# Feed-forward second products one by one in the bank of the sums, and a reordered beginning

## What is computed

```python
h = layernorm(x) * (1 + ca) + sa            # sa, ca, ga, sb, cb, gb: 6 vectors per batch, from silu(c) @ wmod
# attention: causal; each row's scores are first softmaxed within windows of 128 keys,
# and the probabilities so made go through a second softmax over all 1024 keys
x = x + ga * (softmax(window_softmax(q @ k.T / 4)) @ v @ Wo.T + bo)
h = layernorm(x) * (1 + cb) + sb
y = square(relu(h @ Wfc.T)) @ Wproj.T       # 256 -> 1024 -> 256
# five steps: mem = 0.9 * mem + y - (mem > 1);  out = number of steps with mem > 1
x = x + gb * count / 5
```

## Time and profile before

| | |
|---|---|
| median of 3 executions | 2550.83 us (2547.81 to 2559.81) |
| the profiled execution, its own time | 2552.97 us |
| its span from first to last instruction | 2551.1 us |
| mean granted TensorE clock | 0.981 |
| busy: PE, PEld | 2268.9 us (89%), 1266.0 us (50%) |
| busy: DVE, ACT, POOL | 1778.0 us (70%), 1566.2 us (61%), 876.6 us (34%) |
| chain that ended last | PE 70%, DVE 15%, ACT 10%, issue 3%, DMA 1% |

### The profile page before, as it was taken

One profiled execution on the slowest core, in us unless ns is written; L12 is line 12 of the kernel. 1 busy time (PEld: TensorE's weight loads), 2 busy tenths in 40 slices (PEclk: granted clock), 3 DMA queues, 4 the chain that ended last, 5 costly groups with the idle time before them and its releaser, 6 DMA issues.

```text
span 2551.1 us, 46605 instructions
## 1 busy us (share of the span) xinstructions
PE 2268.9 (89%) x19196; PEld 1266.0 (50%) x19196; DVE 1778.0 (70%) x2173; ACT 1566.2 (61%) x2450; POOL 876.6 (34%) x868
## 2 busy tenths in 40 slices
PE   4788889999899998999999998999989998889878
PEld 2434344555455554455544654455545555446537
DVE  4677886777866677876767777667777667777442
ACT  1377676665766567665666657666576656665632
POOL 1243134332533335322443225423253232232324
PEclk8999999999999999999999999999999999999979
DMA  6223122110321114011131013211032111110000
GB/s 187 77 65 106 28 65 85 53 49 12 101 76 28 49 36 127 28 43 36 49 110 53 24 30 93 65 53 49 12 114 63 28 36 32 53 28 7 6 28 17
DMA packets 112241, 140.21 MB, mean 55 GB/s; under 512 B 7912, under 2 KB 83848, under 8 KB 112032
## 3 DMA queue, kind: packets, MB, share of 16 engines
q1 hardware_dynamic: 112032, 137.22, 18.7%
HBM read 74.26 MB, written 58.74 MB: 52 GB/s over the span
## 4 chain that ended last, share of the span: by engine, by line
PE 70%; DVE 15%; ACT 10%; issue 3%; DMA 1%; POOL 0%; SPq 0%; ACTq 0%; POOLq 0%; DVEq 0%
PE sums L610 10%; PE score L555 9%; PE score L562 9%; PE pv L620 8%; PE score L597 8%; DVE negmax L909 7%; PE ring L575 6%; ACT e L805 5%; PE score L508 4%; PE score L525 4%; DVE e L926 4%; PE ring L651 3%; PE score L600 2%; DVE acc L971 1%; ACT qk_f L766 1%
## 5 line engine op out<-in xcount | busy, mean ns | idle before, releaser
L805 ACT ACTIVATE e<-score 128x512 f32<-128x512 f32 x1152 | 673.9, 596 | 343.9 <-PE score L600 206.2
L926 DVE TENSOR_TENSOR e<-ring,e 128x1024 f32<-128x1024 f32 x576 | 680.2, 1222 | 233.5 <-PE ring L651 233.2
L909 DVE TENSOR_REDUCE negmax<-ring 128x8 f32<-128x1024 f32 x512 | 607.3, 1219 | 194.4 <-PE ring L578 193.9
L810 ACT ACTIVATE e<-e 128x1024 f32<-128x1024 f32 x576 | 585.2, 1049 | 6.5 <-DVE e L926 6.1
L597 PE MATMUL score<-q_st,k_st 112*128 112x512 bf16 (+3 forms) x1536 | 462.4, 331 | 107.9 <-ACT qk_p L767 29.1
L575 PE MATMUL ring<-k_st,q_st 96*128 96x512 bf16 (+3 forms) x1536 | 374.7, 329 | 68.0 <-DVE negmax L909 24.0
L1155 POOL TENSOR_SCALAR r_h<-r_b,ab 128x256 bf16<-128x256 f32 x96 | 90.8, 946 | 892.0 <-DVE r_b L932 892.0
L610 PE MATMUL sums<-e,d_ones 128*32 128x256 f32 x4608 | 312.2, 389 | 23.5 <-ACT e L805 17.9
L620 PE MATMUL pv<-e,v 128*17 128x512 f32 (+3 forms) x3072 | 311.4, 494 | 2.9 <-ACT e L810 2.8
L597 PEld LDWEIGHTS score<-q_st,k_st 112*128 112x128 bf16 x1536 | 147.9, 97 | 321.5 <-issue 132.5
L555 PE MATMUL score<-hT,w_fc 128*128 128x256 f32 x1024 | 248.4, 387 | 4.6 <-ACT e L805 3.2
(11 more groups left out here) (123 smaller groups left out, 2521.8 us busy)
## 6 DMA issues: line engine op xcount, KB each, us to landing
q_st<-q_parts SPq DMA_DIRECT2D x32, 768.0 KB, 5.9
k_st<-k_parts SPq DMA_DIRECT2D x32, 768.0 KB, 8.6
q_parts<-qk_p SPq DMA_DIRECT2D x32, 384.0 KB, 2.6
k_parts<-qk_p SPq DMA_DIRECT2D x30, 384.0 KB, 2.6
x_in<-in_x SPq DMA_DIRECT2D x8, 1024.0 KB, 5.5
q_parts<-qk_p SPq DMA_DIRECT2D x32, 256.0 KB, 2.9
x_res<-in_x SPq DMA_DIRECT2D x8, 1024.0 KB, 6.1
out<-acc SPq DMA_DIRECT2D x32, 256.0 KB, 2.2
```

Source lines behind the costliest of these rows:

```text
L805: act.activation(e[:, n % ES, hh, :], score[SCORE_SLOT["st", n, hh][0]][:, :], ACT.Exp, scale=DK ** -0.5).then_inc(e1_done, 1)
L810: act.activation(v, v, ACT.Exp).then_inc(e2_done, 1)
L909: dve.tensor_reduce(negmax[:, hh, 8 * t:8 * t + 8], slot[:, :].rearrange("p (a n) -> p a n", n=P), AX_X, ALU.max, negate=True).then_inc(ri ...
L926: dve.tensor_tensor(v, ring[no % 2][:, :].rearrange("p (i n) -> p i n", i=2), v, ALU.mult).then_inc(ring_free, 1)
```

## The change

1. **F2 is gone as a piece.** Its 8 times 8 products a batch are single products (`quantum`), put by a table (`QUANTA`) at four places of 21 steps between step 22 and step 45 of the batch's back work, 1 to 3 at a place, 46 groups a batch. They accumulate in the right half of the `sums` bank. ACT copies each finished sum out (`take_sum`, 8 a batch); the next sum's first product waits for that copy, and so does the next `sum_unit`.
2. The table of pieces is split into `FRONT` and `BACK`, with other places. Back work now runs over up to 54 steps, so that its end lies in the next period: of a batch, 25 of the 64 products and 4 of the 16 F1 pieces lie beyond step 35.
3. **Spikes are counted on POOL** for all batches but the last, 9 instructions a chunk where DVE had 5. The last batch stays on DVE.
4. The second exponential is one instruction of 128x2048 where it was two. `products` now stand ahead of `sum_unit` in PE's step. POOL's inverse split writes its parts in place. One mask serves for both uses.
5. `x_res` is loaded in four parts, each as soon as the batch before has used its part; the gates are loaded in two; `load_x` comes two steps later.
6. **The beginning:** PE makes only the columns of the first norm ahead of T1; then all 8 QK and 4 V pieces; then the gates and the other columns; then the maxima. DVE splits the first four pieces before it makes the gates. SP stores these parts, loads the stacks of group 0 in two pairs of heads, and only then brings x of batch 1, the other parts and the feed-forward weights. POOL's first copies wait for the norm on DVE.

```diff
@@ tables
+QUANTA = {22: (3, 1, 0, 0), 23: (0, 0, 1, 1), 25: (1, 0, 2, 0), 26: (0, 2, 3, 0), 28: (0, 1, 0, 1), 29: (1, 1, 1, 2), 31: (2, 1, 1, 2), 32: (1, 0, 1, 0), 34: (1, 1, 1, 0), 35: (0, 1, 1, 2), 37: (1, 1, 0, 1), 38: (2, 0, 3, 0), 41: (1, 2, 0, 2), 43: (2, 2, 0, 0), 44: (1, 0, 1, 1), 36: (0, 0, 0, 1), 42: (0, 0, 2, 0), 30: (0, 0, 1, 0), 24: (0, 0, 1, 1), 45: (0, 0, 0, 1), 40: (1, 0, 0, 0)}
...
+def quanta(n):
+
+    out = [[], [], [], []]
+    for r, q in backs(n):
+        at = sum(sum(QUANTA[k]) for k in QUANTA if k < q)
+        for place, count in enumerate(QUANTA.get(q, ())):
+            for no in range(at, at + count):
+                out[place].append((r, no // (2 * NF), no // NF % 2, no % NF))
+            at += count
+    return out
+
+
+def sums_ended(n, place):
+
+    return [(r, c, i) for r, c, i, k in quanta(n)[place] if k == NF - 1]
...
+CHUNK_END = [max(q for q in QUANTA if sum(sum(QUANTA[k]) for k in QUANTA if k < q) < 2 * NF * (c + 1)) for c in range(4)]
+LN2_AT = {13: (0, 1), 14: (2, 3, 4, 5), 15: (6, 7)}
...
+PROLOGUE = [("T1", 0, n) for n in range(4)] + [("QK", 0, n) for n in range(8)] + [("V", 0, n) for n in range(4)]
@@ sync
+            for n in range(4):
+                store_parts(0, n)
+            for par in range(2):
+                sp.wait_ge(stored[par], 96)
+            for pair in range(2):
+                for stacked, dram in ((q_st, part_dram[0]), (k_st, part_dram[1])):
+                    sp.dma_start(stacked[0:KROWS, 0, 2 * pair:2 * pair + 2, :],
...
+            piece_full(sp, "T1", 0, 3)
+            load_x(1)
+            for n in range(4, 8):
+                store_parts(0, n)
...
                     for c in range(4):
+                        if q == max(4, CHUNK_END[c] + 4 - PERIOD):
+                            if r:
+                                sp.wait_ge(fin, 8 * (r - 1) + 2 * c + 2)
+                            sp.dma_start(x_res[:, 2 * c:2 * c + 2, :], x_rows[:, r, 2 * c:2 * c + 2, :]).then_inc(res_in[c], 16)
@@ tensor
-                elif kind == "F2":
-                    c, i = divmod(n, 2)
-                    for f in range(NF):
-                        if i == 0 and f % 2 == 0:
-                            pe.wait_ge(squared, 16 * r + 4 * c + f // 2 + 1)
-                        mm = pe.matmul(ps[:, 0:D], gT[:, f, P * i:P * i + P], w_proj[:, f, :], start=(f == 0), stop=(f == NF - 1))
                 mm.then_inc(piece_ready, 1)
+
+            def quantum(n, r, c, i, f):
+
+                if n % TRI == 0 or n > NUNIT:
+                    pe.wait_ge(r_newton, 2 * (min(n, NUNIT) // TRI - 1) + 1)
+                if f == 0 and (r or c or i):
+                    pe.wait_ge(back_evac, 8 * r + 2 * c + i)
+                if i == 0 and f % 2 == 0:
+                    pe.wait_ge(squared, 16 * r + 4 * c + f // 2 + 1)
+                mm = pe.matmul(sums[:, HALF:HALF + D], gT[:, f, P * i:P * i + P], w_proj[:, f, :],
+                               start=(n > NUNIT and f == 0), stop=(f == NF - 1), skip_group_check=True)
+                if f == NF - 1:
+                    mm.then_inc(back_sum, 1)
...
+                if BACK_ENDED[m + 1]:
+                    pe.wait_ge(back_evac, BACK_ENDED[m + 1])
...
+            for m in range(2):
+                col = 3 * D * m + 2 * D
+                for k in range(NT):
...
+            mm.then_inc(mod_product, 1)
+            columns_of(1)
             for k in range(len(TILES)):
+                if k == 1:
+                    pe.wait_ge(cols_ready, 2)
...
+                if 0 <= n - LAG_P < NUNIT:
+                    products(n - LAG_P)
                 if 0 <= n - 1 < NUNIT:
                     sum_unit(n - 1)
-                if 0 <= n - LAG_P < NUNIT:
-                    products(n - LAG_P)
...
+                for item in single[0]:
+                    quantum(n, *item)
...
+                for item in single[1]:
+                    quantum(n, *item)
@@ scalar
-                elif kind == "F2":
-                    c, i = divmod(n, 2)
-                    if r or c:
-                        act.wait_ge(lif, STEPS * (4 * r + c))
-                    act.activation(n1[:, D * i:D * i + D], ps[:, 0:D], ACT.Copy, scale=-1.0).then_inc(piece_evac, 1)
+
+            def take_sum(r, c, i):
+
+                act.wait_ge(back_sum, 8 * r + 2 * c + i + 1)
+                if i == 0 and (r or c):
+                    act.wait_ge(lif, counted(r, c))
+                act.activation(n1[:, D * i:D * i + D], sums[:, HALF:HALF + D], ACT.Copy, scale=-1.0).then_inc(back_evac, 1)
...
-            def second_exp(m, pair):
-                act.wait_ge(ring_free, RING_NO["r", m, pair] + 1)
-                v = e[:, m % ES, 2 * pair:2 * pair + 2, :]
+            def second_exp(m):
+                act.wait_ge(ring_free, RING_NO["r", m, 1] + 1)
+                v = e[:, m % ES, :, :]
                 act.activation(v, v, ACT.Exp).then_inc(e2_done, 1)
@@ vector
                 if k == 0:
-                    piece_done(dve, "F2", r, 2 * c + 1)
-                    if c == 0 and r + 2 < B:
-                        piece_full(dve, "BT", r + 2, 0)
-                    if r or c:
-                        dve.wait_ge(out_stored, 16 * (4 * r + c))
+                    dve.wait_ge(back_evac, 8 * r + 2 * c + 2)
+                    dve.wait_ge(out_stored, 16 * (4 * r + c))
@@ gpsimd
+            def count_spikes(r, c, k):
+
+                if k == 0:
+                    pool.wait_ge(back_evac, 8 * r + 2 * c + 2)
+                    if r or c:
+                        pool.wait_ge(out_stored, 16 * (4 * r + c))
+                    pool.tensor_scalar(acc[:, :], n1[:, :], -levels[k], None, ALU.is_lt).then_inc(lif, 1)
+                else:
+                    done = counted(r, c) + 2 * k
+                    pool.wait_ge(lif, done - 1)
+                    pool.tensor_scalar(below[:, :], n1[:, :], -levels[k], None, ALU.is_lt).then_inc(lif, 1)
+                    pool.wait_ge(lif, done)
+                    pool.tensor_tensor(acc[:, :], acc[:, :], below[:, :], ALU.add).then_inc(lif, 1)
...
+                            if r < B - 1 and q == CHUNK_END[c] + 1 + k // 2:
+                                count_spikes(r, c, k)
```

More of the change, by code:

```diff
@@ L55 @@
 LAG_R, LAG_E, LAG_P = 5, 6, 7
-LAST = NUNIT + 40
+LAST = NUNIT + 54
 TILES = []
@@ L167, in score_slots @@
     out, held, at = {}, [None, None], 0
-    steps = [[*PROLOGUE, *BESIDE.values(), ("turn", 0, 0)]]
+    steps = [[*PROLOGUE, ("turn", 0, 0)]]
     for n in range(LAST):
@@ L374, in blocks, with counted @@
             return n - LAG_P + 1
-        def backs(n):
-            b = n // PERIOD
-            return [(r, n - PERIOD * (r + 1)) for r in (b - 2, b - 1) if 0 <= r < B]
-        CHUNK_END = [next(at for at, piece in PLACES.items() if piece == ("F2", 2 * c + 1))[0] for c in range(4)]
+        def counted(r, c):
+            return (2 * STEPS - 1) * (4 * r + c) if r < B - 1 else (2 * STEPS - 1) * 4 * r + STEPS * c
         block = ctx.enter_context(nc.Block())
@@ L684, in _ @@
             mm.then_inc(mod_product, 1)
-            pe.wait_ge(gates_made, 1)
+            for m in range(2):
+                col = 3 * D * m + 2 * D
+                for k in range(NT):
+                    mm = pe.matmul(ring[1][0:B, BANK + D * m:BANK + D * m + D], c_s[:, B * k:B * k + B], wmod_sb[:, k, col:col + D], start=(k == 0), stop=(k == NT - 1))
+            mm.then_inc(mod_product, 1)
+            columns_of(1)
             for k in range(len(TILES)):
+                if k == 1:
+                    pe.wait_ge(cols_ready, 2)
                 maxima(0, k)
-                if k in BESIDE:
-                    piece(BESIDE[k])
             turn_maxima(0)
@@ L722, in step @@
                     maxima(*at[1])
+                for item in single[2]:
+                    quantum(n, *item)
                 if n < NUNIT:
@@ L732, in step @@
                     outputs(turned_out(n))
-            pe.wait_ge(ffn_in, 32)
+                for item in single[3]:
+                    quantum(n, *item)
             pe.wait_ge(bias_step, 6)
@@ L1030, in _ @@
             dve.memset(negmax[:, :, :], 0.0)
-            dve.memset(acc[:, :], 0.0)
-            dve.wait_ge(mod_product, 2)
-            dve.tensor_copy(gate_sb, ring[1][0:B, 0:2 * D]).then_inc(mod_own, 1)
+            dve.memset(m_sb[:, :], 0.0).then_inc(zeroed, 1)
+            dve.memset(one[:, :], 1.0)
+            for n in range(4):
+                split_first(n)
+            dve.wait_ge(mod_product, 3)
+            dve.tensor_copy(gate_sb, ring[1][0:B, BANK:BANK + 2 * D]).then_inc(mod_own, 1)
             dve.wait_ge(mod_own, 3)
```

215 lines of the change are left out of this document (114 added, 101 removed), and 10 rows, old and new, of the table PLACES.

## The result

The changed kernel takes 2436.16 us, median of four executions in the comparison; the kernel before 2549.32 in the same one. One of the four took 4367.98 us, with no trace to say why, and is left out of the ratio (the median of the other three is 2435.94). The profiled execution took 2435.94 us, its span 2434.2.

A forecast was written before the change was run, and what follows sets the result against it. TensorE was taken to bound the middle, with at most 22.9 us to win in each of seven periods. Terms -32 - 14 - 16 + 23 = -39 gave 2514 us for the profiled execution, 2512 against the median; range 2465 to 2556.

The forecast's parts named there:

- The middle (-32): Single products, step order and merged exponential: 66 us of waits go, 34 of costs come; bounds +34 and -105.
- The bank's hand-over (+10): In the sums' bank, three of a batch's eight sums wait for ACT's late copy, 0.4 us each: +10 us.
- The order (17.9 us of waits): In PE's step, products with v ahead of the sums cover 17.9 us of waits for ACT's last exponential.
- The exponential (nothing): On ACT, merging the second exponential into one instruction a unit was costed at nothing, as ACT has slack.
- DVE's relief (11): Spike counts leaving DVE take away a third of PE's waits for ring banks that DVE reads: 11 us.
- Work moved later (-14): Period 1 gets shorter by 14 us, bounds -18 and -8; the work added to the last stage falls into idle PE.
- The beginning (-16): First tiles start 9 us earlier and 7 us go before the first scores: -16 us, bounds -8 and -20.
- The end (+23): Last stage: POOL's counts make it 19 us late, the dense feed-forward 4 more; bounds +8 and +35.
- (b): Rival, chance 0.15: in the middle an even feed removes most waits, as 3.5 us blocks starve ACT and DVE; 2457 us.
- (a): Rival, chance 0.15: PE's waits in the middle only move to the next bank; only ends and period 1 count; 2544 us.
- (c): Rival, chance 0.10: POOL's queue becomes the bound, deciding from 2.8 us a comparison on; 2576 us at 3.5.
- (d): Rival, chance 0.05: DVE and POOL share a port, slowing the splits of maxima, 24 x 0.7 us; 2529 us.

The follow-up runs named there:

- number 10: Changed kernel with sums first, second exponential in halves, all spikes counted on DVE, and F2 products in blocks of eight in a score bank: 2550.18 us.
- number 2: Changed kernel with F2's products in blocks of eight, last in eight steps, in a score bank as in the kernel before: 2527.74 us.
- number 11: Changed kernel with each step's one to six single products together as that step's last item: 2520.72 us.
- number 1: Changed kernel with F2's products in blocks of eight, last in eight steps, still in the sums' bank: 2532.59 us.
- number 3: Changed kernel with the sums ahead of the products with v again: 2474.42 us.
- number 4: Kernel before with the products with v put ahead of the sums: 2530.25 us, ratio 0.9928.
- number 8: Changed kernel with the spikes of batch 6's last two chunks counted on DVE in place of POOL: 2420.37 us, ratio 0.9494.
- number 7: Changed kernel with all spikes counted on DVE, none on POOL: 2444.16 us.
- number 14: number 8 with the second norm's statistics moved later, behind DVE's split of the maxima: 2417.49 us, ratio 0.9478.
- 6: Kernel before with the second exponential merged into one instruction a unit: 2558.90 us, ratio 1.0028.
- 15: number 14 with seven steps' last-place single products moved into the gaps between scores: 2424.92 us.
- 5: Changed kernel with the second exponential in two halves again: 2446.24 us.
- 9: Changed kernel with sums first, second exponential in two halves and all spikes counted on DVE: 2476.63 us.
- 12: Changed kernel with each step's single products together between its third and fourth scores: 2476.35 us.
- 13: Changed kernel with each step's single products together between its first and second scores: 2518.83 us.

## Why the prediction was wrong

**The middle (-32).** This is the step that failed: the waits that the sum takes away (66 us) and the costs that it sets against them (34). The changed kernel is 134 us below number 10 over periods 0 to 7, against 32, and past the bound of 105. Three things in the sum were wrong. (1) *Which waits go.* I gave the F2 copy's bank 14.8 us and half of two others; the bank is worth nothing by itself (number 2), the copy's wait was one for a count that came too soon after another, and the single products fill gaps at other bank waits too: spread over their places in the step they are worth 84 us more than at its end (number 11), where the sum took half of two waits. (2) *The ceiling.* "At most 22.9 us of each of seven periods" took busy PE as a floor, but it fell by 4.8 us: short waits hide in modelled ends, as in step 26. Period 2 won 17.7 us and stayed under 22.9, but the bound of two thirds of it did not hold. (3) *The costs.* The sum has 16 us for entries into float32 (38 x 8 x 0.05 is 15); the steps compared here show none. Step 4 of period 2 has one single product in the changed kernel and none in number 1:

```profile
634.98:643.81 8.83, 8.83 (x71) 5.53 (x67) 5.94 (x6) 6.05 (x8) 8.41 (x8) 1.00 0.40 103
```

```profile
648.73:657.28 8.55, 8.55 (x70) 5.11 (x66) 5.94 (x6) 5.94 (x8) 8.20 (x7) 1.00 0.33 103
```

It adds 0.28 us, where a product is 0.43 in the dense end; steps 7 and 8, with four and three more than in number 1, are 0.40 and 0.43 us longer. The bank's hand-over (+10) would be real with sums first (number 3), but the new order, which I had counted as another gain, is what hides it.

**The order (17.9 us of waits).** In the kernel before it gives 18.5, but the number is partly luck: about half of the waits stood in periods 0 and 7, and in the full periods the gain was twice the wait, less what drops of the clock took back (number 4). In the changed kernel it gives 38, in part for the reason just told. **The exponential (nothing):** right for the kernel before, 10 us in the changed one. **DVE's relief (11):** 24 in periods 2 to 6 alone, through the addition ahead of the products as much as through the ring's banks.

**Work moved later (-14).** Number 10 has 14.0 us in period 1; to the figure is luck, as the same run's periods 2 to 6 are 7 us longer than before for the new places, of which period 1 has its share. What failed is the other half, "the added work in the last stage falls into idle PE": it adds 17.4 us there.

**The beginning (-16).** Measured -13.4, with period 0 another -3.4. The first tile came 13 us earlier, not 9, but the second then waited 3.02; the first scores at 81.71 stand where "near 80" had them. No run takes the edits of the beginning apart.

**The end (+23).** Measured +36.5: 17.6 for the counts up to T2 (number 8), where 19 was taken; 4.9 behind T2, where 4 was taken; and 14.0 ahead of T2 that stay without the counts, where the moved work was taken as free. So the counts' term was right, and the term at nothing was the wrong one.

**The rivals.** (b), at 2457, came nearest, and was right in its direction. Its mechanism, blocks of 3.5 us that starve ACT, was only a small part: blocks of one to six, last in their steps, cost 84 of the 96 us. (a) fell. (c) did not come: a comparison is 1.49 us, below the 2.8 from which it would decide, and PE's wait for POOL's squares is 3.8 us in all. (d): DVE's second operation of a split takes between 0.87 and 1.60 us in both kernels, 1.59 in step 16 of period 2, where POOL runs all the while; its median is 1.51 us in the kernel before and 0.89 in the changed one. The Trainium skill (SBUF — State Buffer, Who interferes with whom) says that a VectorE instruction with two SBUF inputs contends with a GpSimd instruction that reads SBUF; the trace agrees. What is new is that PE waits for the split, 12.6 us in periods 1 to 7. The 1.3 us of step 16 stand in number 7 too, which has no count on POOL, so it is not the counts that cause them.

With the terms as measured (-134 for the four parts in periods 0 to 7, +8 for the new places, -14 and +17 for the moved work, -13 for the beginning, +19 for the rest of the last stage, 154.59 - 135.47) the sum is -117, the difference of the two spans. It has to be, since the terms are differences of stages over number 10; it orders the 117 us and does not test their causes.

## What to carry to other kernels

Where PE alternates with a slower reader over two banks, look for the gaps between its groups, and give PE independent products there; the same products at the end of the step brought 12 of 96 us here. In the third gap alone they brought 44 more, spread over four places all 96; whether small groups or more gaps did the rest is open. Don't take busy PE as a floor, and don't price such waits one by one: moving the products from the end of the step to the third gap also took the wait behind the turned maxima from 12.4 to 3.1 us. Remove the parts of a change together as well as singly, since here they sum to 182 us apart and 134 together.

## What was not expected of the hardware

The granted clock can fall after waits of about a microsecond, and need not. Step 16 of period 2 has the same two waits, 1.3 and 0.77 us, in the changed kernel and in number 1 (first the changed one):

```profile
729.20:738.45 9.25, 7.14 (x73) 3.57 (x68) 7.03 (x18) 5.87 (x11) 3.93 (x5) 1.00 0.30 99
```

```profile
746.13:757.07 10.94, 8.83 (x73) 4.11 (x69) 7.02 (x18) 5.91 (x11) 3.96 (x5) 0.84 0.25 84
```

At a mean of 0.84 of the clock, so with a stretch at 1.2 GHz, it is 1.69 us longer: there the four products of a QK piece take 3.64 us, and in the other kernel 1.98. In number 14 two of the five such steps of periods 2 to 6 have the drop (284.32 and 284.31 us, the others 282.61 and 282.62). So periods of one kernel come in lengths 1.7 us apart, with the same instructions; what decides is not shown.

The drops in periods 2 to 6 of the profiled executions: none in the changed kernel and in number 8; one in 6 and 15; two in 5, 7 and 14; three in the kernel before, 3 and 9; four in 10 and 11; five in 12; six in 13; seven in 4; ten in 1 and 2 (one of double length is counted as two). In the kernel before they are 1.4 to 1.7 us each. So up to 17 of the 85 us by which number 1's periods 2 to 6 are longer, and some 7 of 66 in number 11, are the clock. A wait taken away may thus give more than itself, but no run here separates the two.
